# A cross-attention and feed-forward block: the probabilities are normalised on VectorE instead of GpSimd

## The reference

```
scores = einsum('bhqd,bhkd->bhqk', Q, K) * scale - slope[h] * (query_pos - key_pos)
scores = where(mask == 0, -inf, scores)
m      = max(scores, axis=-1)
e      = exp(scores - m)
attn   = e / (1.0 + sum(e, axis=-1))          # the division that the change moves
out    = einsum('bhqk,bhkd->bhqd', attn, V) @ W_o.T
x      = x + tanh(g_xattn) * out              # Q comes from layernorm(x), K and V from the context
...
xr, xk = mixes of layernorm(x) with its shifted copy, by mu_r and mu_k
x      = x + tanh(g_ffn) * sigmoid(xr @ W_r.T) * (square(relu(xk @ W_k.T)) @ W_v.T)
```

## Time and profile before

| what | us |
|---|---|
| median of 3 runs (1510.21 to 1513.52) | 1513.15 |
| the profiled execution | 1510.14 |
| its span, first to last instruction | 1508.3 |
| first `bias` of batch 0, of batch 1, of the last batch | 98.04, 179.85, 1401.63 |
| PE busy, DVE busy, ACT busy, POOL busy | 1394.9, 1160.7, 888.2, 721.8 |

### The profile page before, as it was taken

One profiled execution on the slowest core, in us unless ns is written; L12 is line 12 of the kernel. 1 busy time (PEld: TensorE's weight loads), 2 busy tenths in 40 slices (PEclk: granted clock), 3 DMA queues, 4 the chain that ended last, 5 costly groups with the idle time before them and its releaser, 6 DMA issues.

```text
span 1508.3 us, 32873 instructions
## 1 busy us (share of the span) xinstructions
PE 1394.9 (92%) x10864; PEld 1096.0 (73%) x10864; DVE 1160.7 (77%) x2889; ACT 888.2 (59%) x2928; POOL 721.8 (48%) x766
## 2 busy tenths in 40 slices
PE   7989899999999999998999999999999999899898
PEld 6876768677676867667676766777686677768667
DVE  4457878787987868798786879878686887868775
ACT  5147474756747475674737566574756657474662
POOL 0004555555455554555555464545555455455542
PEclk9999999999999999999999999999999999999999
DMA  8722011020100102020110202010010201011000
GB/s 268 217 70 49 8 29 50 0 77 0 56 20 28 49 10 67 0 56 20 36 41 14 63 0 56 20 52 25 26 51 0 64 12 56 20 28 49 1 29 28
DMA packets 53009, 65.95 MB, mean 44 GB/s; under 512 B 23024, under 2 KB 29168, under 8 KB 52976
## 3 DMA queue, kind: packets, MB, share of 16 engines
q1 hardware_dynamic: 52976, 65.52, 14.6%
HBM read 40.87 MB, written 24.64 MB: 43 GB/s over the span
## 4 chain that ended last, share of the span: by engine, by line
DVE 34%; PE 26%; issue 20%; POOL 9%; ACT 5%; DMA 4%; DVEq 1%; SPq 1%; POOLq 0%; ACTq 0%
PE rotating L401 19%; DVE probs L1039 5%; DVE diff L1101 4%; POOL square L1358 4%; DVE mix_k L1096 4%; DVE relu L1101 2%; PE probs_bank L561 2%; DVE square L1096 2%; PE score_bank L401 2%; DVE mask_in L1138 2%; POOL xnt_or_act L1360 2%; DVE xs L1065 2%; DVE stats L1009 2%; DMA xs<-in_x_dram 2%; ACT probs L774 2%
## 5 line engine op out<-in xcount | busy, mean ns | idle before, releaser
L774 ACT ACTIVATE probs<-probs,neg_max 128x120 f32<-128x120 f32 x1024 | 391.5, 387 | 32.9 <-DVE neg_max L1043 32.9
L1321 POOL TENSOR_TENSOR probs<-probs,recip 128x960 f32<-128x960 f32 x128 | 229.8, 1795 | 225.6 <-DVE recip L1054 225.6
L401 PE MATMUL rotating<-mixed_key,w_key 128*128 128x512 f32 x720 | 213.7, 441 | 43.3 <-ACT gated L826 43.3
L401 PE MATMUL rotating<-w_proj,attn_t 128*128 128x512 f32 x768 | 207.5, 409 | 20.7 <-ACT gated L826 18.7
L401 PE MATMUL rotating<-w_value,xnt_or_act 128*128 128x512 f32 x720 | 203.5, 411 | 15.5 <-DVE xs L1065 10.3
L782 ACT COPY probs_t<-probs_bank 120x512 f32<-120x512 f32 x256 | 149.8, 585 | 110.9 <-PE probs_bank L561 110.5
L1039 DVE SCALAR_TENSOR_TENSOR probs<-mask_in,score_bank 128x120 f32<-128x120 f32 x1024 | 213.5, 271 | 0.0
L401 PEld LDWEIGHTS rotating<-mixed_key,w_key 128*128 128x128 f32 x720 | 141.7, 209 | 80.9 <-ACT gated L826 49.7
L401 PE MATMUL rotating<-xnt_or_act,w_query 128*128 128x256 f32 x1536 | 198.7, 286 | 0.5 <-DVE xnt_or_act L1024 0.5
L774 ACT ACTIVATION_READ_ACCUMULATOR probs<-probs,neg_max 128x1 f32 x1024 | 196.1, 191 | 0.0
L401 PE MATMUL rotating<-w_gate,mixed_gate 128*128 128x512 f32 x768 | 189.6, 399 | 0.0
(11 more groups left out here) (126 smaller groups left out, 2131.6 us busy)
## 6 DMA issues: line engine op xcount, KB each, us to landing
xs<-in_x_dram SPq DMA_DIRECT2D x64, 256.0 KB, 2.9
out_dram<-gated SPq DMA_DIRECT2D x64, 256.0 KB, 3.0
value_scratch<-gated SPq DMA_DIRECT2D x16, 240.0 KB, 2.7
mask_in<-in_mask_dram SPq DMA_DIRECT2D x16, 240.0 KB, 2.7
keys_t<-key_scratch SPq DMA_DIRECT2D x16, 240.0 KB, 3.6
values<-value_scratch SPq DMA_DIRECT2D x16, 240.0 KB, 3.7
probs<-in_ctx_t_dram SPq DMA_DIRECT2D x6, 480.0 KB, 7.1
key_scratch<-query_t SPq DMA_DIRECT2D x12, 240.0 KB, 4.9
```

The lines of the kernel that those rows point to most:

```text
L401: mm = pe.matmul(bank, stationary(a, c), moving(b, c), start=(i == 0), stop=(i == MATMULS - 1))
L774: e = act.activation(probs[:, t % 2, head, :], probs[:, t % 2, head, :], ACT.Exp, bias=neg_max[:, t % 2, head:head + 1], accum_out=sums[:, ...
L1321: pool.tensor_tensor(part, part, recip[:, t % 2, heads].unsqueeze(2).to_broadcast((P, H // 2, NK)), ALU.mult)\
```

## The change

Eight instructions per batch, 128 in all, leave POOL's list and enter DVE's. In DVE's list each stands directly behind the reciprocal that it reads, with a wait of DVE on its own `recip_ready`. Operands, shape and data type stay the same, and so do the semaphore that PE waits for and its counts. Nothing else is moved; the lists of PE, ACT and SP are the same.

```diff
             def reciprocals(b, t, half):
...
                 dve.wait_ge(sum_ready, at)
                 dve.reciprocal(recip[:, t % 2, heads], sums1[:, t % 2, heads]).then_inc(recip_ready, 1)
+                part = probs[:, t % 2, heads, :]
+                dve.wait_ge(recip_ready, at)
+                dve.tensor_tensor(part, part, recip[:, t % 2, heads].unsqueeze(2).to_broadcast((P, H // 2, NK)), ALU.mult)\
+                    .then_inc(probs_ready, 1)
...
-            def normalise_probs(b, t, half):
-                heads = slice(half * H // 2, (half + 1) * H // 2)
-                pool.wait_ge(recip_ready, (b * QT + t) * 2 + half + 1)
-                part = probs[:, t % 2, heads, :]
-                pool.tensor_tensor(part, part, recip[:, t % 2, heads].unsqueeze(2).to_broadcast((P, H // 2, NK)), ALU.mult)\
-                    .then_inc(probs_ready, 1)
...
-                normalise_probs(b, 0, 0)
                 feed_forward((squared_relu, 0))
-                normalise_probs(b, 0, 1)
                 feed_forward((squared_relu, 1), (squared_relu, 2), (squared_relu, 3))
-                normalise_probs(b, 1, 0)
-                normalise_probs(b, 1, 1)
                 rstd2_of(b, 0)
-                normalise_probs(b, 2, 0)
                 after((rstd1_of, 0))
-                normalise_probs(b, 2, 1)
                 edge(b, 0)
                 difference(b, 0)
                 rstd2_of(b, 1)
-                normalise_probs(b, 3, 0)
-                normalise_probs(b, 3, 1)
                 after((rstd1_of, 1))
```

## The result

The changed kernel takes **1561.66 us** (median of 4 runs, 1560.80 to 1562.57) against 1513.34 (4 runs, 1510.21 to 1514.22) for the kernel before on the same chip: a ratio of **1.0328, interval 1.0315 to 1.0341**, slower by 48.3 us. The prediction was 1552, range 1532 to 1576. The profiled execution took 1562.57, with a span of 1560.3 against 1508.3.

A forecast was written before the change was run, and what follows sets the result against it. DVE's list was taken to set the pass in the stretch up to the residual, PE close behind; 14 passes of 2.6 us plus 2.5 for the outer batches, about 39 us, gave 1552 us, range 1532 to 1576.

The forecast's parts named there:

- the dearer case: Rival: nothing gained early, 1.28 per multiplication, one POOL meeting per pass; 4.8 us per pass, 1583; chance 0.13 for 3.4 or more.
- What one multiplication costs: On DVE, each moved multiplication costs 1.17 us including 0.10 for its reciprocal's end, ends 1.07 and 1.28; broadcast operand free.
- The two halves of tile 0: nothing: Tile 0's two multiplications cost DVE nothing, since they fit into its 5.29 us wait for ACT's exps before 726.97.
- gains in the first stretch: Before 726.97, PE's waits of 0.52 and 0.36 go, so DVE starts about 0.9 us earlier; ends 0 and 1.2.
- Cost from 726.97 on: Up to the residual at 762.38, six multiplications cost 7.02 us, less gains 2.42, with POOL meetings 2.6 per pass.
- the three reliefs: DVE's delays beside POOL that go: finish 0.86, first mix 1.52, layer norm 0.60; together 2.98 us per pass.
- The 0.2 for meetings with POOL: Allowance of 0.2 us per pass for DVE's new multiplications being held up by POOL's remaining short instructions.
- the case against the change: All six multiplications lose to a POOL instruction of 1.04 us: 4.8 us more per pass, some 67 us in all.
- PE doesn't escape: ACT's exps of tile 3 wait longer for DVE's maxima, so PE is 2.2 us later by 745, then waits for the residual.
- Sum: 14 passes of 2.6 give 36.4 us, with the outer batches 39 us; 1549 profiled, 1552 as median.
- Outer batches: First and last batch outside the 14 passes: 2.0 us in batch 0 and 0.5 in the last.
- PE as the bound: Rival: PE bounds, DVE follows, and all that PE's waits lose is kept: 12 us faster, 1501; chance 0.07.

The follow-up runs named there:

- tile 0 alone without the gap: Only tile 0's two multiplications moved to DVE and three covered waits taken out, against the kernel before: 1498.51 us, ratio 0.9908.
- the control: The kernel before with only the same covered waits of DVE taken out: 1511.89 us, ratio 0.9995.
- the merged distances alone: The kernel before with DVE's four distance subtractions of 128x120 made one: 1505.62 us, ratio 0.9957.
- the memsets: The kernel before with eight tiny memsets added to DVE's list, in every batch: 1531.31 us; in batch 0 only: 1531.25 us.

## Why the prediction was right, and what it missed

The sign, the place of the larger loss and its mechanism were right, and the time lay in the range. The 1552 came out 9.7 too low, and that is the difference of two errors: the body was made too dear by some 5 us (39 against 33.6), and a loss of some 15 us was not in the sum. That the time lies in the range is in part luck: the room above 1552 was kept for the dearer case, none of whose terms came, and the loss at the turn took it.

- **What one multiplication costs**: 1.17 was a little high. From the sums to tile 0's residual there is one multiplication and nothing else new: 3.39 us after against 2.27 before (from starts at 22.61 and 26.00 in the pass after, 23.43 and 25.70 before), so 1.12. The broadcast operand costs nothing: 1158 ns against the 1156 of the earlier trace rows.
- **The two halves of tile 0: nothing**, and **gains in the first stretch**, 0.9: borne out in size by tile 0 alone without the gap, 0.69 earlier at the sums and 0.83 in the pass, and by the changed kernel, 0.82. But it was read from the pass at 703.54, one of the two in 14 with PE at full clock in this stretch; the passes are alike in length, not in PE's waits there. At that clock the gain is 1.17, and what is measured is a mixture over the passes' clocks, which the forecast does not have. That it comes near 0.9 is luck.
- **Cost from 726.97 on**: the wait of 0.72 went, and the three reliefs came as read, to 0.01 (0.86, 1.51, 0.60). With the measured 1.12 and 0.82: 6 x 1.12 - 0.82 - 0.72 - 2.97 = 2.21; measured 2.18 at the residual. The 0.2 for meetings with POOL came to nothing: no multiplication was held up, and where one met POOL's short instruction, that one lost (1.45 in place of 0.57). The rule of the Trainium skill (SBUF — State Buffer, § Who interferes with whom) that whoever starts first wins holds on both kernels, by these rows; the case against the change that was drawn from it, six losses of DVE, needs POOL to be first, and POOL was released by DVE's own instructions just ahead.
- **PE doesn't escape**: right. ACT's wait for the maxima grew by 1.34 where 2.2 was read, but PE's value product still waits for the residual (0.74).
- **Sum**: this step fell short in what it left out. The 14 x 2.6 = 36.4 for the passes should have been 14 x 2.15 = 30.1, and there is no term in it for the turn of the loop, 14 x 1.20 = 16.8 in the trace (14.7 by the two medians). The added code was priced by its time on the engine only; that eight more instructions in batch 0 and eight in the body push the body's end over a place from which it is fetched at every turn could not be read from any row of before, but the instruction queue's 14 packets were in the page, and the code's growth in the diff.
- **Outer batches**, 2.5: not settled. By the spans the profile of after has 52.0 - 46.9 = 5.1 outside the passes, by the medians it is 1.4. Batch 0 took 81.81 us before and 84.69 in the control with the same work, so a single profile can't tell this term.
- **Rivals**: PE as the bound fell (no multiplication at all gains 1.70 a pass, putting six on DVE loses 2.15). The dearer case's lower end came close in size, 3.35 against 3.4 per pass, by none of its own mechanisms: the start was early, a multiplication cost 1.12, and none lost to POOL.

## What to carry to other kernels

Before an instruction is moved to another engine, sort its copies by what stands in front of each: those behind a long wait are free (tile 0: 0.8 us a pass won), those in a full stretch cost their length less the delays that they spare there, and tile 3's second half was worth it (1.12 for 1.51) while the other five together lose 3.19 a pass (89.35 - 86.16). Moving those three halves, taking out the covered waits and merging one stage gives 1484.73 us where moving all gave 1561.66. And when code is added to an engine that loops, look at the first instruction of each pass for idle time that nothing releases, and at the count of instruction packets: here eight tiny ones, inside the loop or in front of it, cost 19 us.

## What was not expected of the hardware

- The jump back of DVE's loop costs no idle time or 1.1 to 1.4 us, by where the body lies in the program: 0.23 to 0.30 us or 2.7 to 3.0 from the jump to the sequencer's next record, 13 to 15 packets of instruction DMA or 78 to 79. Eight tiny instructions outside the loop turned one into the other, for 19.2 us.
- PE's granted clock at the start of a pass is not the same in all passes of one execution: over the first 7.5 us it was 0.54 to 1.00 in the 14 passes of the kernel before (mean 0.77, 1.00 in two of them), 0.58 to 0.89 in those of the changed kernel (mean 0.71), and 1.00 in 12 of 14 in the version of 1484.73 us. PE's wait for ACT just ahead of the stretch was 2.9 us in the first two and 2.45 in the last; but with the merged distances alone it was 2.46 too, and the clock 1.00 in only 6 of 14. What sets the clock there stays open; the gap alone doesn't, since with the memsets it was 0.84 to 0.86 in 13 of them.
- Of a multiplication on DVE and a 128x1 power on POOL that started 0.13 us after it, DVE lost nothing (1157 to 1162 ns in all 128) and POOL 0.88 us.
